# Attention: the short rows' products with the values in plain fp32, one head in each half of the array's columns

## The reference, cut to the stage that is changed

Two transformer-like layers over x of 2 x 1024 x 256. The change touches only the first attention: 16 heads of 64 share one key and one value matrix, with a bias of 16 x 1024 x 1024, a causal mask, a padding mask and one extra "null" key and value.

## Time and profile before

| | |
|---|---|
| device time, three runs | 1053.42 us median (1050.03 to 1053.71) |
| span of the profiled execution | 1055.2 us |
| mean granted clock of PE over the span | 0.925 |
| attention stage | about 44 to 617 us |
| busy over the span: PE, DVE, ACT, POOL | 932.6, 803.2, 735.9, 606.0 us |
| 320 `pT_lo` on DVE (L2508), 320 `pT_hi` on ACT (L2403) | 202.5 us, 175.5 us |
| 576 + 576 products with the values on PE (L2610, L2611) | 175.0 us, 150.4 us |

### The profile page before, as it was taken

How to read it: one execution, slowest core, us unless ns; L and a number is a source line. 1 busy time by engine, 2 the same in 40 slices (tenths; PEclk the granted TensorE clock), 3 DMA queues, 4 the chain that set the end, 5 groups by cost and what they waited for, 6 DMA issues and landing times. The chain is left out here.

```text
span 1055.2 us, 22432 instructions
## 1 busy us (share of the span) xinstructions
PE 932.6 (88%) x6180; PEld 811.6 (77%) x6180; DVE 803.2 (76%) x2324; ACT 735.9 (70%) x1651; POOL 606.0 (57%) x699
## 2 busy tenths in 40 slices
PE   7899999999999999999999966887976762599997
PEld 5578888888888898998888755677964652499996
DVE  7579989899898898998888879774757786344443
ACT  2268888888888998998999937434764652466663
POOL 2368777777776666775555525481066277344444
PEclk8879999999999999999999986888988885699999
DMA  9156656666666566675665440155864523254453
GB/s 309 44 175 180 189 171 189 178 181 180 176 184 182 170 197 182 187 199 167 182 189 171 137 150 1 51 167 148 282 178 157 205 102 138 88 78 78 73 84 48
DMA packets 111427, 162.14 MB, mean 154 GB/s; under 512 B 16201, under 2 KB 85193, under 8 KB 110282
## 3 DMA queue, kind: packets, MB, share of 16 engines
q1 hardware_dynamic: 100200, 140.56, 45.1%
q0 software_dynamic: 10224, 18.00, 8.2%
q10 hardware_dynamic: 882, 2.14, 0.6%
HBM read 110.31 MB, written 25.17 MB: 128 GB/s over the span
## 5 line engine op out<-in xcount | busy, mean ns | idle before, releaser
L2375 POOL TENSOR_SCALAR probs<-probs,inv_sum 128x1024 f32<-128x1024 f32 (+3 forms) x128 | 301.7, 2370 | 174.2 <-DVE inv_sum L2526 174.2
L2421 ACT ACTIVATE probs<-probs,neg_max 128x1025 f32<-128x1025 f32 (+7 forms) x256 | 197.5, 772 | 30.9 <-DVE neg_max L2486 29.8
L2508 DVE TENSOR_TENSOR pT_lo<-t_ps,pT_hi 128x512 fp32r<-128x512 f32 (+1 forms) x320 | 202.5, 633 | 21.3 <-ACT pT_hi L2403 20.8
L2590 PE MATMUL t_ps<-ident,probs 128*128 128x128 f32 x1152 | 179.9, 274 | 1.1 <-DVE pT_lo L2508 1.1
L2610 PE MATMUL o_ps<-pT_hi,values 128*128 128x256 f32 x576 | 175.0, 323 | 5.2 <-DVE pT_lo L2508 3.5
L2403 ACT ACTIVATE pT_hi<-t_ps 128x512 fp32r<-128x512 f32 (+1 forms) x320 | 175.5, 549 | 5.5 <-PE t_ps L2590 2.3
L2486 DVE CUSTOM_DVE_ANT_0 probs<-s_ps,bias_set,neg_null 128x512 f32<-128x512 f32 (+3 forms) x256 | 164.2, 642 | 4.5 <-PE s_ps L2559 2.6
L2590 PEld LDWEIGHTS t_ps<-ident,probs 128*128 128x128 f32 x1152 | 141.9, 141 | 31.4 <-DVE pT_lo L2508 2.7
L2611 PE MATMUL o_ps<-pT_lo,values 128*128 128x256 f32 x576 | 150.4, 281 | 0.0
L2558 PE MATMUL s_ps<-k_hi,q_hilo 128*128 128x512 f32 (+3 forms) x384 | 143.8, 375 | 4.2 <-PEq L2730 1.4
L2559 PE MATMUL s_ps<-k_lo,q_one 128*128 128x512 f32 (+3 forms) x384 | 135.4, 353 | 0.0
(11 more groups left out here) (385 smaller groups left out, 2124.7 us busy)
## 6 DMA issues: line engine op xcount, KB each, us to landing
bias_set<-bias_dram SPq DMA_DIRECT2D x16, 1024.0 KB, 5.5
bias_set<-bias_dram SPq DMA_DIRECT2D x16, 896.0 KB, 5.4
bias_set<-bias_dram SPq DMA_DIRECT2D x16, 768.0 KB, 4.9
bias_set<-bias_dram SPq DMA_DIRECT2D x16, 640.0 KB, 4.7
q_hilo<-q_hi SPq DMA_DIRECT2D x128, 64.0 KB, 2.0
q_hilo<-q_lo SPq DMA_DIRECT2D x128, 64.0 KB, 2.0
q_one<-q_hi SPq DMA_DIRECT2D x128, 64.0 KB, 2.0
bias_set<-bias_dram SPq DMA_DIRECT2D x16, 512.0 KB, 5.5
```

The lines of the kernel that those rows point to most:

```text
L2375: last = pool.tensor_scalar(keys, keys, inv_sum[:, x.set, unit, h:h + 1], None, ALU.mult)
L2421: act.activation(p, p, ACT.Exp, scale=-1.0, bias=neg_max[:, x.set, row.unit, h:h + 1], accum_out=row_sum[:, x.set, row.unit, h:h + 1]).the ...
L2508: dve.tensor_tensor(pT_lo[n % 3][:, 0:count, :], t_ps[TURNS["slot", n] % 3][:, 0:2 * P * count].rearrange("p (n q) -> p n q", n=count), pT ...
L2590: last = pe.transpose(t_ps[at % 3][:, P * (2 * m + h):P * (2 * m + h) + P], probs_row(x, row, h)[:, 1 + P * (k + m):1 + P * (k + m) + P], ...
```

```diff
         self.pT_lo = [sbuf(st, f"pT_lo{i}", [P, 2, 2 * P], F32R) for i in range(3)]
+        self.pT_whole = [sbuf(st, f"pT_whole{i}", [P, 2, 2, P]) for i in range(3)]
...
+        def lows(n):
+            g, i = divmod(n, SLOTS_A_STEP)
+            return sum(len(x.rows[0].slots) for x in ALL[:g]) + min(i, len(ALL[g].rows[0].slots))
+
+        def turns_read(pe, at):
+            if at < 0:
+                return
+            kind, n = TURN_AT[at]
+            if kind == "null":
+                pe.wait_ge(t_read, lows((n + 1) * UNIT_SLOTS - 1) + n + 1)
+                return
+            x, i = slot_of(n)
+            if x.slots[i][0].unit:
+                pe.wait_ge(hi_out, n + 1)
+            else:
+                pe.wait_ge(t_read, lows(n) + 1 + x.round)
...
 ACT, high(n):
+                    if row.unit:
+                        act.activation(pT_whole[n % 3][:, 0:count].rearrange("p n h q -> p (n h q)"), turned, ACT.Copy).then_inc(hi_out, 1)
+                    else:
+                        act.activation(pT_hi[n % 3][:, 0:count, :], turned, ACT.Copy).then_inc(hi_out, 1)
 ACT, outputs(x, row):
+                    if row.unit:
+                        return
...
 DVE, low(n):
+                    if row.unit == 0:
+                        dve.wait_ge(hi_out, n + 1)
+                        dve.tensor_tensor(pT_lo[n % 3][:, 0:count, :], ...
 DVE, outputs(x, row):
+                    if row.unit:
+                        dve.wait_ge(pv_done, SLOTS_A_STEP * (x.g + 1))
+                        dve.tensor_copy(oT[1][:], o_ps[1][:, 0:P]).then_inc(oT_ready, 1)
+                        return
...
 PE, turn(n):
-                    wait(pe, t_read, at - 2)
+                    turns_read(pe, at - 3)
 PE, weigh(n):
-                    pe.wait_ge(t_read, TURNS["slot", n] + 1)
+                    turns_read(pe, TURNS["slot", n])
                     for m in range(count):
+                        if row.unit:
+                            for h in range(2):
+                                last = pe.matmul(o_ps[1][DH * h:DH * h + DH, 0:P], whole_values[:, QT * x.batch + k + m, :], pT_whole[n % 3][:, m, h, :],
+                                                 start=(k + m == 0), stop=(k + m == row.blocks - 1), skip_group_check=True)
+                            continue
...
 ACT, values_high(g), ahead of the stage:
                         act.activation(values[:, 4 * g:4 * g + 4, 0:DH], vps[g % 2][:, :, 0:DH], ACT.Copy).then_inc(v_out, 1)
+                        act.activation(whole_values[:, 4 * g:4 * g + 4, :], vps[g % 2][:, :, 0:DH], ACT.Copy).then_inc(v_out, 1)
 DVE, values_low(g), ahead of the stage:
-                        dve.wait_ge(v_out, g + 1)
+                        dve.wait_ge(v_out, 2 * (g + 1))
```

More of the change, by code:

```diff
@@ L2237, in __init__ @@
         self.pT_lo = [sbuf(st, f"pT_lo{i}", [P, 2, 2 * P], F32R) for i in range(3)]
+        self.pT_whole = [sbuf(st, f"pT_whole{i}", [P, 2, 2, P]) for i in range(3)]
         self.oT = [sbuf(st, f"oT{i}", [P, P]) for i in range(2)]
-        self.o_low = [sbuf(st, f"o_low{i}", [DH, 2 * P]) for i in range(2)]
+        self.o_low = sbuf(st, "o_low", [DH, 2 * P])
     def bias_row(self, x, row):
@@ L2264, in attention_stage @@
 def attention_stage(nc, sbuf, psum, sem, bias, keep):
-    ident, xnT, xs, x, x_again, yacc, wq_all, k_hi, k_lo, values, wo, neg_null, null_wo, tiles, bias_in, bias_ready, q_in = keep
+    ident, xnT, xs, x, x_again, yacc, wq_all, k_hi, k_lo, values, whole_values, wo, neg_null, null_wo, tiles, bias_in, bias_ready, q_in = keep
     with ExitStack() as st:
@@ L2283, in attention_stage @@
         pT_lo = tiles.pT_lo
+        pT_whole = tiles.pT_whole
         oT = tiles.oT
@@ L2402, in high @@
                     act.wait_ge(turn_ready, n + 1)
-                    act.activation(pT_hi[n % 3][:, 0:count, :], t_ps[TURNS["slot", n] % 3][:, 0:2 * P * count], ACT.Copy).then_inc(hi_out, 1)
-                def outputs(x, row):
-                    wait(act, oT_ready, units_done(x.g, row.unit) - 2)
-                    act.wait_ge(pv_done, SLOTS_A_STEP * x.g + (len(x.rows[0].slots) if row.unit == 0 else SLOTS_A_STEP))
-                    act.activation(o_low[row.unit][:], o_ps[row.unit][DH:P, :], ACT.Copy).then_inc(o_low_ready, 1)
+                    turned = t_ps[TURNS["slot", n] % 3][:, 0:2 * P * count]
+                    if row.unit:
+                        act.activation(pT_whole[n % 3][:, 0:count].rearrange("p n h q -> p (n h q)"), turned, ACT.Copy).then_inc(hi_out, 1)
+                    else:
+                        act.activation(pT_hi[n % 3][:, 0:count, :], turned, ACT.Copy).then_inc(hi_out, 1)
+                def outputs(x, row):
+                    if row.unit:
+                        return
+                    wait(act, oT_ready, units_done(x.g, 0) - 2)
+                    act.wait_ge(pv_done, SLOTS_A_STEP * x.g + len(x.rows[0].slots))
+                    act.activation(o_low[:], o_ps[0][DH:P, :], ACT.Copy).then_inc(o_low_ready, 1)
                 def query(g):
@@ L2506, in low @@
                     row, k, count = x.slots[i]
-                    dve.wait_ge(hi_out, n + 1)
-                    dve.tensor_tensor(pT_lo[n % 3][:, 0:count, :], t_ps[TURNS["slot", n] % 3][:, 0:2 * P * count].rearrange("p (n q) -> p n q", n=count),
-                                      pT_hi[n % 3][:, 0:count, :].bitcast(F32), ALU.subtract).then_inc(t_read, 1)
+                    if row.unit == 0:
+                        dve.wait_ge(hi_out, n + 1)
+                        dve.tensor_tensor(pT_lo[n % 3][:, 0:count, :], t_ps[TURNS["slot", n] % 3][:, 0:2 * P * count].rearrange("p (n q) -> p n q", n=count),
+                                          pT_hi[n % 3][:, 0:count, :].bitcast(F32), ALU.subtract).then_inc(t_read, 1)
                     if (n + 1) % UNIT_SLOTS == 0:
@@ L2517, in outputs @@
                     wait(dve, projected, units_done(x.g, row.unit) - 2)
-                    dve.wait_ge(o_low_ready, units_done(x.g, row.unit))
+                    if row.unit:
+                        dve.wait_ge(pv_done, SLOTS_A_STEP * (x.g + 1))
+                        dve.tensor_copy(oT[1][:], o_ps[1][:, 0:P]).then_inc(oT_ready, 1)
+                        return
+                    dve.wait_ge(o_low_ready, x.g + 1)
                     for h in range(2):
                         cols = slice(P * h, P * h + P)
-                        last = dve.tensor_tensor(oT[row.unit][DH * h:DH * h + DH, :], o_ps[row.unit][0:DH, cols], o_low[row.unit][:, cols], ALU.add)
+                        last = dve.tensor_tensor(oT[0][DH * h:DH * h + DH, :], o_ps[0][0:DH, cols], o_low[:, cols], ALU.add)
                     last.then_inc(oT_ready, 1)
@@ L2621, in project @@
                     if x.pair == PAIRS - 1 and row.unit == 1:
-                        pe.wait_ge(t_read, TURNS["null", x.round] + 1)
+                        turns_read(pe, TURNS["null", x.round])
                         for unit in range(2):
@@ L3000, in _ @@
                     values_and_null_scores(3)
-        attention_stage(nc, sbuf, psum, sem, bias, (ident[:], xnT, xs, x, x_again, yacc, wq_all, k_hi, k_lo, values, wo, neg_null, null_wo, tiles, bias_in, bias_ready, q_in))
+        attention_stage(nc, sbuf, psum, sem, bias, (ident[:], xnT, xs, x, x_again, yacc, wq_all, k_hi, k_lo, values, whole_values, wo, neg_null, null_wo, tiles, bias_in, bias_ready, q_in))
         attn.close()
```

2 lines of the change are left out of this document (added).

## The result

The change made the kernel a little slower: 1057.7 us median (20 runs, 1053.41 to 1063.26) against 1053.83 for the kernel before (20 runs beside it), a ratio of 1.0042 with a 95% interval of 1.0024 to 1.0059. The profiled execution spans 1061.4 us against 1055.2, at a mean granted clock of 0.921 against 0.925. The forecast was 1055, with a range of 1043 to 1084.

A forecast was written before the change was run, and what follows sets the result against it. The attention step was taken as bound by a 4.4 us relay across PE, ACT and DVE plus 4.1 us of PE. Terms 0, 0, +4, -2 for one to four short blocks and +0.3 at the start gave +2: 1055 us, range 1043 to 1084.

The forecast's parts named there:

- The relay: Attention step: query, q_hi on ACT, long exponential, DVE's reciprocal, scores; PE waits for this chain, 4.4 us a step.
- the slack: PE's spare time inside a step: 0.4, 0.5, 0 and 0.45 us for one, two, three, four short blocks.
- Rival 2: Attention steps all fall to PE's need because DVE and ACT have less to do: -10 us, 1043; chance 0.16.
- Streams: PE, short block: loses two records (-0.24), gains two overlapping fp32 matmuls at 0.22, net -0.02 us; upper bound +0.20.
- Rival 1: PE, short blocks: the two heads' matmuls do not overlap, +0.20 more a block; +27 us, 1081; chance 0.32.
- Switches: PE, 96 short slots: entering and leaving the other array partition costs 0.15 us a slot, bounds 0.05 to 0.18.
- rival 3: PE, short slots: halves overlap but each switch costs a record's whole tail, 0.32 a slot; +12 us, 1066; chance 0.10.
- Rounds with three short blocks: Attention, 16 steps without slack: PE gains +0.24 us a step, +4 us in all.
- Rounds with four: Attention, 16 steps: PE +0.22, relay gives up 0.45 a step, half of it counted; -2 us in all.
- DVE and ACT: Attention stage: low halves -57 us, short outputs -18, ACT's copies -24; DVE's busy time falls by some 75 us.
- Start: Start of the attention stage: a second copy of the values ahead of DVE's low half, +0.3 us for the last group.
- The sum: Whole kernel: all terms together, +2 us on the profiled execution's 1055.2, 1.8 above the runs' median; forecast 1055 us.

The follow-up runs named there:

- experiment 1: Kernel before without DVE's low halves for short slots, TensorE multiplying the values with pT_hi twice instead; 1044.51 us, ratio 0.9931.
- experiment 2: Changed kernel with both heads' short products in the same half of the columns, so they cannot overlap; 1094.78 us, ratio 1.038.

## Why the prediction was right, and where not

**The relay, and the slack.** Right. I put the slack at 0.4, 0.5, 0 and 0.45 us; experiments 1 and 2 give 0.40, 0.52, about 0.07 (1.30 added, 1.23 paid) and 0.35. So one and two short blocks cost nothing, as forecast. Rival 2 (the relay gives way everywhere, 1043) falls: less work on DVE leaves 8.51 and 8.59 as they are (experiment 1).

**Streams.** Right at the end I took: 0.22 a block, the heads side by side. Rival 1 (no overlap, 1081) falls; experiment 2 is what it described, and took 1094.8, more than rival 1 gave, as it pays the dearer switches too. The Trainium skill ("TensorE: Matmul & The Clock Gate", Measured speedup vs the span model) has three column tiles of 32 columns run 2.38 times faster together. These runs agree in kind: two 64-column tiles run twice as fast as one behind the other (0.22 against 0.44).

**Switches: the term that was mis-sized.** I took 0.15 a slot, with bounds of 0.05 to 0.18; it is 0.35, above the upper bound and close to what rival 3 described (0.32, a record's whole tail on each side). I had read it from the null key's forms, and read them wrongly: the same trace already held the price. The record that follows the two turns there is the query's first:

```profile
137.84 1.06 PE L2568 MATMUL s_ps<-xs,wq_all 128*128 128x128 f32 x8
```

From 135.99 to 137.84 are 1.86 us by the trace's nanoseconds. The records in between stream for 6 x 0.216 + 2 x 0.109 = 1.51, so the visit of the 16-row form costs 0.34. I counted 0.09 ahead of it and 0.09 behind it. I left out 0.10 between its first two records, which start 0.32 apart and not 0.22 (with 0.22 throughout, `t_ps` could come at 137.39; my 137.48 has that 0.10 in it), and 0.06 between the two turns behind it. It is 0.34 in all seven such visits inside the stage. The 0.05 at 544.96 was no price of its form: with the change the 16-column form follows the transposes by 0.11, one stream time, in six of eight rounds.

The parts are alike in the slot of one block: 0.09 ahead of the first pair (0.20 for 0.11), 0.05 between the pairs' starts (0.16 for 0.11), 0.10 from the last pair's start to the scores (0.21 for 0.11) and 0.11 between their two records (0.34 for 0.23), 0.35 in all. The last 0.11 is what PE also pays behind a wait. In the kernel before, the second record behind the wait at 98.95 comes 0.34 later as well:

```profile
99.29 0.39 PE L2559 MATMUL s_ps<-k_lo,q_one 128*128 128x512 f32 x1
```

So a visit looks as if PE started anew on both sides of it. I had taken the 0.09 to agree in kind with a full drain, though it is less than the 0.16 of a record's tail; what the runs show is the time, near two such tails, and not what happens inside. The Trainium skill ("TensorEngine Tiling (Array Packing)", Available Configurations) lists 128x128 and 128x64 as different configurations of the array; what going from one to the other costs, these runs had to measure.

**Rounds with three short blocks.** +4 forecast, +6.5 measured. With 0.35 it would have been (0.70 - 0.06 - 0.07) x 16 = +9. The twelve steps inside a round paid just that, 0.56 each, but the four at the ends of the two rounds took 37.6 us together where they took 37.8. The relief of DVE alone takes 1.0 off those four (experiment 1); what gives the rest there stays open.

**Rounds with four.** -2 forecast, -0.1 measured, by two errors that cancel. In the steady step 0.70 - 0.08 of PE meets a slack of 0.35: +0.27, where I had -0.1. But the stage's last four steps, which have no queries left to make (the last two no scores either), took 23.7 us instead of 26.1, a term that I left out. There PE waited for DVE (the kernel before):

```profile
612.79 0.39 PE L2610 MATMUL o_ps<-pT_hi,values 128*128 128x256 f32 x1 [0.55 <-DVE pT_lo L2508]
...
614.75 0.70 PE L2619 MATMUL y_ps<-wo,oT 128*128 128x256 f32 x2 [0.44 <-DVE oT L2521]
```

Now one wait of 0.36 for `oT` is left there. Experiment 1, with the relief alone, has 24.3 for the same four steps.

**DVE and ACT.** Low halves -57.3 (I had 57), outputs -17.5 (18), ACT's `o_low` -24.5 (24). DVE's busy time fell by 61, not 75: records that overlap by 0.08 at their ends are counted once there. Start +0.5 (0.3), everything behind the stage unchanged: right.

**The time.** The sum was +2 and the measured ratio is +4.4 us (2.5 to 6.2). Between the two profiled spans it is +6.2; against the terms of the sum that is a difference of +2.5 with three short blocks, +1.9 with four, -1.1 with one and two, +0.2 at the start and +0.4 behind. The relay, the slack and the overlap held; the price of the switch did not, and that 1055 came so near is in part luck. With 0.35 a slot the same sum has +9 with three short blocks and 0.27 x 16 = +4 with four, 1067, close to rival 3's 1066, and the usual periods (8.51, 8.60, 8.61, 8.82) are nearer to what rival 3's sum gives (8.5, 8.6, 8.6, 8.7) than to the 8.25 and 8.45 that I gave for three and four blocks. The ends of rounds and the last four steps, which I had not priced, gave most of that back.

## What to carry to other kernels

Packing two 64-column matmuls into one array does halve their stream, but each visit to that tiling costs 0.35 us here, so it pays only where a visit holds a good deal of work: put the visits together, or stay out of it in the steps that have no slack. Taking 57 us of work off DVE bought 8 us of the stage (experiment 1), 5.8 of it in the rounds with four short blocks, where they stood on the relay in the usual step and ahead of PE's waits in the last four. Read the price of a form over its whole visit, from the last ordinary record ahead of it until the stream is regular again, and not at its two edges alone. Price a resource from its own slack, kind of step by kind of step, and price the ends of rounds and the winding down of a pipeline apart. The order of instructions can matter more than their work: one product a step moved by one slot cost 4%, 44 us, where the 96 visits to the other tiling take 34 us of PE's time.

## What the runs showed of the hardware that was not expected

- A visit to 128x64 tiles between full-width fp32r matmuls costs PE 0.35 us, at 1, 2 or 4 blocks a visit (1.24 and 1.40 against 0.90 and 1.09, 1.90 for 1.54; 0.36 back for one visit less), with or without overlap of the halves. Plain fp32 at full width in the same place costs nothing beside its stream (1.48 = 1.09 + 0.39). The 16-row form of the null key costs the same as the narrow tiles, 0.34 a visit; the 16-column form costs nothing.
- The records of two such tiles start 7 ns apart. The second pair of a visit follows after 0.16, each further one after 0.11, the stream time of one record.
- A record of PE behind a switch, or behind a wait, is followed by its next one late (0.34 for 0.23 at 512 columns), so a short wait costs more than the gap that it shows.
